# Decoder layer on one core: residual x1 kept in seven tiles of 128 tokens in place of eight of 112

## The chip, the cores and the metric

One NeuronCore of a Trainium2 chip runs the whole kernel. The metric is the device time of one execution in microseconds (us), the median of several.

## The reference

One pre-norm decoder layer on x of shape 8 x 112 x 512 (896 tokens) in float32, with a context of 8 x 375 x 512:

```python
x = x + attn(ln(x))                      # 16 heads of 32, rotary, causal, Wqkv with bias
x = x + xattn(ln(x), ctx)                # ln once more, with weights; then
    # q, k, v = fp8 linears of the tokens (16, 8, 8 heads of 128), LN per head, GQA within a sequence
    # qx = fp8 linear of the tokens; kx, vx = linear of ctx, LN on qx and kx, GQA over the 375
    # out = (fp8-rounded concat of both, 4096) @ wproj.T * scale
x = x + ffn(ln(x))                       # ternary weights, per group of 64
    # h = silu(gate) * up (2048); rms_norm(h) @ w_proj.T
```

The output is a float32 tensor of 8 x 112 x 512.

## The kernel before

The 896 tokens are worked on by batch: `NB` = 8 sequences of `T` = 112 tokens. The residual `x1` lies in SBUF as eight blocks of 112 partitions x 512. Where a matmul has the tokens as its weight columns, there are 112 of them, and the matmul streams 512 columns.

Phase A (up to about 225 us, `run_a`) normalises each batch, does its causal attention, adds it to x1 (`a_s4`, L640), normalises again (`l_0` to `l_2`) and quantises the tokens for the four linears (`l_q`, `quant`). Beside it the weights of S0 are prepared (`s0prep`): SP fetches blocks of 512 KB into four staging buffers, ACT casts them to bf16 (`b_0`, L326 and L328), and DVE or POOL forms the low part (`b_1`, L337 and L339).

The main loop goes by ticks. It runs four halves: S0 and S1 (self-attention by groups, heads 0 to 7 and 8 to 15) and X0 and X1 (the same over the context). A batch takes four ticks in S and eight in X. `p_mm` projects the tokens (L845, L855), `lnb_z` and `lnb_t` normalise and transpose (L785, L796), `t_s0` makes scores and exponentials (L935, L942, L947, L950), `t_s1` scales (L967), `t_s2` transposes and copies (L979, L996), `t_s3` multiplies by v (L1014), `t_s4` quantises four heads at a time into the buffer `cat` (`quant`: four DVE operations L655 to L658, then two on POOL, L659 and L660), and `t_s6` projects `cat` of a batch by 16 matmuls of 512 columns (L1052) and adds the result to x1 (L1058). Each stage runs a fixed number of ticks behind the first (`order`): `t_s4` five, `t_s6` eight. The weights of the next half are prepared in the same ticks, in X0 and X1 also the ternary weights of the FFN, half of which go out to DRAM through `spill_ring` and come back.

The FFN: `f_0` to `f_2` normalise and transpose x1 batch by batch (L1071, L1080, L1089, L1090) as soon as X1 has finished a batch; the first six come together after the last projection of queries. `g_0` and `g_1` do gate and up for 448 tokens at a time, 16 blocks of each (`j` = 0 among the last batches of X1, then `j` = 1): L1119, Silu on ACT L1128, product L1137, high and low part L1139 and L1140, squares summed on POOL L1145 and L1146. `d_0` and `d_1` do the down projection of a batch by 32 matmuls of 512 columns (L1168), its RMS factor (L1173, L1176, L1179) and the last sum (L1184), and SP stores it.

The order on each engine is the order in which the program emits: five queues, each strictly in order, with semaphores between them. SP has one queue, `sync_items`; an entry that waits holds up all behind it (`run_dma`).

Of the kernel before, what the change touches and what calls it, by code (L numbers as in the profile page):

```python
# [120 lines left out]
def decoder_layer(nc, x, ctx_t, w_a, w_s, w_x, w_p, w_g, w_d, vec, bias, cst, cst2, scr, out):  # L121
    ctx = ExitStack()
    with ctx:
# [59 lines left out]
        aFR = rings.take(1024)  # L183
        fr = Ring([f32(aFR + 512 * i, 512) for i in range(2)])
# [6 lines left out]
        catr = Ring([b16(rings.take(448), 896).rearrange("p (h t) -> p h t", h=8) for _ in range(2)])  # L191
# [263 lines left out]
        x1tok = [None] * NB  # L455
        A = [dict(b=b) for b in range(NB)]
# [167 lines left out]
        def a_s4(g):  # L624
# [17 lines left out]
            x1tok[b] = t3  # L642

# [5 lines left out]
        def quant(src, mul, dst, toks, free_dst):  # L649
# [10 lines left out]
            t5 = pool(lambda e: e.tensor_tensor(dst, t3, m3, ALU.subtract), t4, free_dst)  # L660
# [33 lines left out]
        def l_q(it, vs, last):  # L694
# [3 lines left out]
            for v in vs:  # L698
                dst = xqx[:, :, T * b:T * b + T] if v == 3 else xqv[:, v, :, T * b:T * b + T]
                mul = rsc[:, 4 * v:4 * v + 4].unsqueeze(2).broadcast_to([128, 4, T])  # L700
                t1, t5 = quant(f3, mul, dst, [tf, t_rsc], None)
# [104 lines left out]
        def proj_items():  # L806
            items = []
            for hf in halves:
                for b in range(NB):
                    bt = dict(hf=hf, b=b, ready=[], k=hf["kind"])  # L810
                    hf.setdefault("batches", []).append(bt)
                    bt["n"] = 4 if hf["kind"] == "S" else 8
# [210 lines left out]
        def t_s4(it):  # L1023
# [4 lines left out]
            if g == 1:  # L1028
                bt["cat"] = catr.take()
                bt["tcat"] = []  # L1030
            _, cat, cfree = bt["cat"]
# [5 lines left out]
            t1, t5 = quant(bk[:, 0:448].rearrange("p (h t) -> p h t", h=4), mul, cat[:, h0:h0 + 4, :],  # L1037
                           [it["tpv"], t_rsm], cfree)
            bank.release(bi, t1)
            bt["tcat"].append(t5)  # L1040

        def t_s6(it):
            if not it["last"]:
# [12 lines left out]
            catr.release(ci, t)  # L1056
# [4 lines left out]
            x1tok[b] = t2  # L1061
# [6 lines left out]
        def f_0(b):  # L1068
            si, rr, tr = ln_rstd(ln_stats(x1[:, b, :], T, 1, 512, x1tok[b]))
            zi, z, zf = zr.take()  # L1070
            th = act(lambda e: e.activation(z[0:T, :], x1[0:T, b, :], ACT.Identity, bias=rr[0:T, 1:2],  # L1071
                                            scale=rr[0:T, 0:1]), tr, zf, x1tok[b])
# [3 lines left out]
        def f_1(b):  # L1076
            zi, z, th = F[b]
            bi, (bk, _), free = bank.take()
            for k in range(4):
                t = pe(lambda e, k=k: e.transpose(bk[:, T * k:T * k + T], z[0:T, 128 * k:128 * k + 128],  # L1080
                                                  identf[0:T, 0:T]), th, free, signal=k == 3)
# [3 lines left out]
        def f_2(b):  # L1085
            bi, bk, t = F[b]
            b4 = bk[:, 0:448].rearrange("p (k t) -> p k t", k=4)
            sl = slice(T * b, T * b + T)
# [7 lines left out]
        ffn_h = [[], []]  # L1096
        spots = [
            [PW[0] + 3584 + 224 * m for m in range(16)],
            [PW[0] + 7168 + 224 * m for m in range(4)] + [X_CT + 224 * m for m in range(6)]
            + [X_K0 + 224 * m for m in range(6)],  # L1100
            [PW[0] + 8192 + 224 * m for m in range(16)],
            [aKV + 224 * m for m in range(13)] + [X_V0 + 224 * m for m in range(3)],
        ]
        for j in range(2):
            ffn_h[j] = [(b16(spots[2 * j][m], 448), b16(spots[2 * j + 1][m], 448)) for m in range(16)]
        acc = [f32(aXQX, 448), f32(a_att, 448)]
        sq = Ring([f32(aXQX + 448, 448)])
        hf_ring = Ring([f32(aXQX + 896 + 448 * i, 448) for i in range(2)] + [f32(X_V0 + 672, 448)])
        wg = b16(PW[1], 4 * 4096).rearrange("p (k n) -> p k n", k=4)
        wd = b16(PW[1] + 8192, 16 * 512).rearrange("p (m n) -> p m n", m=16)  # L1110
        def g_0(it):
            m, j = it["m"], it["j"]
            toks = [t for b in range(4 * j, 4 * j + 4) for t in xTtok[b]]
            for which in range(2):
                bi, (bk, _), free = bank.take()
                n = 0
                for k in range(4):
                    for s in range(2):
                        t = pe(lambda e, k=k, s=s, n=n, bk=bk, which=which: e.matmul(  # L1119
                            bk[:, 0:448], wg[:, k, 2048 * which + 128 * m:2048 * which + 128 * m + 128],  # L1120
                            xT[:, s, k, 448 * j:448 * j + 448], start=n == 0, stop=n == 7),
# [4 lines left out]
            i, h, hfree = hf_ring.take()  # L1126
            after = free_at[j]
            ts = act(lambda e: e.activation(h, bk[:, 0:448], ACT.Silu), t, hfree, after)  # L1128
# [3 lines left out]
        def g_1(it):  # L1132
# [4 lines left out]
            th = dve(lambda e: e.tensor_tensor(h, h, bk[:, 0:448], ALU.mult), t, it["ts"])  # L1137
# [5 lines left out]
            else:  # L1143
                qi, q, qf = sq.take()
                tq = pool(lambda e: e.tensor_tensor(q, h, h, ALU.mult), th, qf, after)  # L1145
# [12 lines left out]
        outs = []  # L1158

        def d_0(it):  # L1160
            b = it["b"]
            j = b // 4
            sl = slice(T * (b % 4), T * (b % 4) + T)
# [237 lines left out]
```

How the kernel before makes its waits and increments, by code:

```python
    def emit(self, eng):  # L63
        for need, make, inc in self.items:
            last = {}
            for t in need:
                last[id(t.sem)] = t
            for t in last.values():
                eng.wait_ge(t.sem, t.value)
            ins = make(eng)
            if inc:
                ins.then_inc(self.sem, 1)
# [1229 lines left out]
        def run_dma(eng, items):  # L1302
            for waits, dst, src, s in items:
                for t in waits:
                    eng.wait_ge(t.sem, t.value)
                eng.dma_start(dst, src).then_inc(s, 16)
# [1 line left out]
        @block.sync  # L1308
        def _(eng):
            run_dma(eng, sync_items)
            eng.wait_ge(s_out, 16 * NB)
```

## Time and profile before

| | |
|---|---|
| median of 3 runs | 1261.43 us (1261.06 to 1262.6) |
| profiled execution, its own time | 1259.75 us |
| its span | 1257.9 us |
| granted clock of TensorE, mean | 0.977 |
| PE, DVE, ACT, POOL busy | 95%, 75%, 64%, 48% of the span |
| HBM | 51 GB/s on average |

PE is TensorE's matmul stream and PEld its weight loads, DVE is VectorE, POOL is GpSimd, SP issues the DMAs. Records of matmuls overlap, as one starts before the one ahead of it has drained; their distance from start to start is what a stream costs. In a timeline the columns are start (us), length (us), engine, line, operation, output, input, count, and in brackets how long the engine had stood idle and what ended that. In the view by stretch they are the stretch, its length, then each engine's busy us with the number of instructions, the granted clock, the share of the DMA engines and GB/s. The view of a line gives count, ns at least, median and at most, first and last start. A DMA line ends with KB of one and median us from issue to landing.

### The profile page before, as it was taken

The page shows a single profiled execution, that of the slowest core. Times are in us where ns is not written, and L with a number is a line of the kernel's source. Part 1 is how long each engine was busy: PE and PEld are TensorE (multiplying, and loading weights), DVE is VectorE, ACT ScalarE, POOL GpSimd, SP SyncE. Part 2 cuts the span into 40 slices and gives each one's busy share as a digit, 9 for nine tenths or more (in the row PEclk, how much of TensorE's full clock was granted, in tenths as well). Part 3 has the DMA queues.
Part 4 walks back from the last instruction along what each step waited for, and adds up shares of the span by engine and source line. Part 5 has one row for each costly group of instructions (what it writes and reads, how often), then busy time and mean ns, then how long its engine had stood idle before and what let it go on. Part 6 is the DMA issues. An engine that isn't in the chain of part 4 may idle for free.

```text
span 1257.9 us, 19385 instructions
## 1 busy us (share of the span) xinstructions
PE 1195.8 (95%) x6408; PEld 819.4 (65%) x6432; DVE 938.0 (75%) x2794; ACT 805.3 (64%) x2301; POOL 607.8 (48%) x722
## 2 busy tenths in 40 slices
PE   4999989889999999999999999999999997999998
PEld 2677767566676666667666677766767765565545
DVE  4679987999888887899999866667777877463341
ACT  4676557777877776577666675667777767652230
POOL 2538875643544545465455632224544443363470
PEclk9999988899999999999999999999999999899999
DMA  8230000011211121212323211041101100000000
GB/s 264 86 99 18 2 1 1 1 51 51 67 35 34 59 80 47 92 44 91 104 88 109 82 47 38 17 142 59 50 27 59 59 18 1 1 1 16 15 1 30
DMA packets 25460, 65.60 MB, mean 52 GB/s; under 512 B 2720, under 2 KB 8992, under 8 KB 25360
## 3 DMA queue, kind: packets, MB, share of 16 engines
q1 hardware_dynamic: 25088, 64.00, 16.2%
q8 instruction: 51, 0.84, 0.3%
q14 instruction: 49, 0.40, 0.1%
q10 hardware_dynamic: 272, 0.36, 0.1%
HBM read 59.37 MB, written 4.98 MB: 51 GB/s over the span
## 4 chain that ended last, share of the span: by engine, by line
PE 47%; DVE 27%; ACT 19%; POOL 4%; issue 2%; DMA 1%; ACTq 0%; POOLq 0%; SPq 0%
PE ps L855 9%; PE ps L1052 8%; PE ps L1119 8%; ACT big L785 6%; PE ps L845 4%; PE ps L1168 4%; PE ps L1014 3%; PE ps L947 3%; DVE big L412 3%; DVE big L967 3%; ACT big L950 2%; PE ps L979 2%; DVE big L240 2%; DVE big L655 2%; DVE big L656 2%
## 5 line engine op out<-in xcount | busy, mean ns | idle before, releaser
L855 PE MATMUL ps<-big 128*125 128x512 bf16 x1152 | 264.5, 379 | 0.5 <-ACT big L942 0.5
L785 ACT ACTIVATE big<-ps,big 112x128 f32<-112x128 f32 (+1 forms) x512 | 192.4, 456 | 72.6 <-POOL big L430 70.1
L855 PEld LDWEIGHTS ps<-big 128*125 128x125 bf16 x1152 | 155.2, 136 | 80.3 <-ACT big L942 0.8
L429 POOL TENSOR_TENSOR big<-big 112x4 f32<-112x4 f32 (+1 forms) x128 | 38.6, 302 | 319.7 <-ACT big L424 319.7
L845 PE MATMUL ps<-big 128*112 128x512 bf16 x768 | 187.4, 387 | 1.9 <-ACT big L942 1.0
L659 POOL TENSOR_TENSOR big<-big 128x448 f32<-128x448 bf16 x96 | 102.8, 1071 | 111.1 <-DVE big L964 70.1
L845 PEld LDWEIGHTS ps<-big 128*112 128x112 bf16 x768 | 99.8, 132 | 65.8 <-issue 6.4
L967 DVE TENSOR_SCALAR big<-big 112x112 f32<-112x112 f32 (+1 forms) x256 | 131.5, 534 | 6.8
L412 DVE BATCH_NORM_STATS2 big<-ps 112x6 f32<-112x128 f32 (+1 forms) x512 | 113.3, 283 | 20.1 <-PE ps L855 18.8
L1014 PE MATMUL ps<-big 125*128 125x224 f32 (+1 forms) x512 | 122.1, 362 | 5.5 <-DVE big L996 4.8
L950 ACT ACTIVATE big<-ps,big 112x375 f32<-112x375 f32 x128 | 74.6, 583 | 82.3 <-DVE big L949 81.2
L1052 PE MATMUL ps<-big 128*112 128x512 bf16 x512 | 116.0, 379 | 3.2 <-ACT big L942 3.2
L660 POOL TENSOR_TENSOR big<-big 128x448 bf16<-128x448 f32 x96 | 111.6, 1163 | 7.5
L947 PE MATMUL ps<-big 128*112 128x375 f32 x256 | 103.5, 486 | 0.5 <-DVE big L657 0.5
L1014 PEld LDWEIGHTS ps<-big 125*128 125x128 f32 (+1 forms) x512 | 92.9, 194 | 16.7 <-DVE big L996 5.9
L979 PEld LDWEIGHTS ps<-big 112*125 112x125 f32 (+1 forms) x512 | 79.6, 177 | 29.0 <-DVE big L967 3.8
L1119 PE MATMUL ps<-big 128*128 128x448 bf16 x512 | 98.3, 352 | 0.0
L949 DVE TENSOR_REDUCE big<-ps 112x1 f32<-112x375 f32 x128 | 68.3, 534 | 39.1 <-PE ps L947 38.2
L1052 PEld LDWEIGHTS ps<-big 128*112 128x112 bf16 x512 | 65.3, 130 | 48.7 <-issue 7.8
L802 ACT ACTIVATE big<-ps,big 128x448 f32<-128x448 f32 (+1 forms) x128 | 94.3, 737 | 0.0
L979 PE MATMUL ps<-big 112*125 112x112 f32 (+1 forms) x512 | 85.7, 269 | 2.7 <-DVE big L967 1.5
L504 PE MATMUL ps<-big 128*112 128x512 bf16 x288 | 76.4, 415 | 5.1 <-DVE big L240 3.5
(115 smaller groups left out, 2312.4 us busy)
## 6 DMA issues: line engine op xcount, KB each, us to landing
big<-in_ctx_t SPq DMA_DIRECT2D x32, 375.0 KB, 3.7
big<-in_w_s SPq DMA_DIRECT2D x16, 512.0 KB, 3.6
big<-in_w_p SPq DMA_DIRECT2D x16, 512.0 KB, 3.7
big<-in_w_x SPq DMA_DIRECT2D x16, 512.0 KB, 3.8
big<-in_w_g SPq DMA_DIRECT2D x16, 512.0 KB, 3.7
big<-in_w_d SPq DMA_DIRECT2D x8, 512.0 KB, 4.6
big<-in_w_a SPq DMA_DIRECT2D x8, 384.0 KB, 4.6
scr<-big SPq DMA_DIRECT2D x24, 128.0 KB, 1.7
```

What stands on the lines that cost most here:

```text
L412: t = dve(lambda e, j=j: e.bn_stats(st[:, j, :], src[0:rows, width * j:width * j + width]), toks, free)
L659: t4 = pool(lambda e: e.tensor_tensor(t3, y3, m3, ALU.add), t2)
L660: t5 = pool(lambda e: e.tensor_tensor(dst, t3, m3, ALU.subtract), t4, free_dst)
L785: t = act(lambda e, j=j: e.activation(z[0:rows, 128 * j:128 * j + 128], bk[0:rows, 128 * j:128 * j + 128], ACT.Identity, bias=rr[0:rows, 4 ...
L845: t = pe(lambda e, k=k, s=s, n=n: e.matmul(bk[0:T, :], xq[:, k, :], w[:, s, k, col:col + 512], start=n == 0, stop=n == 7), xq_tok[(v, b)], ...
L855: t = pe(lambda e, k=k, s=s, u=u, n=n: e.matmul(bk[0:CK, :], cT[:, s, k, CK * c:CK * c + CK], w[:, u, k, col:col + 512], start=n == 0, sto ...
L947: t = pe(lambda e: e.matmul(bk[0:T, 0:SC], q[:, h, :], kk[:, g, :], start=True, stop=True), bt["ready"], free)
L967: tl = dve(lambda e, j=j: e.tensor_scalar(hl[0:T, w * j:w * j + w], p[0:T, w * j:w * j + w], ri[:, j:j + 1], None, ALU.mult), tr, hf)
L979: t = pe(lambda e, j=j: e.transpose(bb[0:rows, T * j:T * j + T], hl[0:T, rows * j:rows * j + rows], identf[0:T, 0:T]), it["tl"], free, sig ...
L1014: t = pe(lambda e, c=c: e.matmul(bk[:, o:o + 224], v[0:rows, c, 128 * g:128 * g + 128], pT[0:rows, 224 * c:224 * c + 224], start=c == 0, s ...
L1052: t = pe(lambda e, h=h, s=s, n=n: e.matmul(bk[0:T, :], cat[:, h, :], hf["wp"][:, s, h, :], start=n == 0, stop=n == 15), bt["tcat"], free, ...
L1119: t = pe(lambda e, k=k, s=s, n=n, bk=bk, which=which: e.matmul(bk[:, 0:448], wg[:, k, 2048 * which + 128 * m:2048 * which + 128 * m + 128] ...
```

## The change

After phase A has finished a batch of x1, SP stores it to a DRAM buffer `xs` of 896 x 512. Once the stores that cover 128 rows have landed and the old block has been read, it loads them into `x1t`, seven tiles of 128 tokens in the same SBUF. The attention stays by batches of 112; `quant` can write to several places, and `t_s4` writes the heads of a batch to one or two tiles of `cat` (two on POOL for batches 1 to 6). `t_s6` projects tile b-1 at the end of batch b, so nothing at the end of batch 0. There are three `cat` buffers in S and two in X. The FFN's norm, its down projection and the stores of the output go by these seven tiles; gate and up take 512 and 384 tokens in place of 448 and 448. The third `cat` buffer is the place of x1's eighth block, later used for the spill ring and for an FFN buffer.

```diff
-        aFR = rings.take(1024)
-        fr = Ring([f32(aFR + 512 * i, 512) for i in range(2)])
+        aFR = rings.take(896)
+        fr = Ring([f32(aFR + 448 * i, 448) for i in range(2)])
+        aCX = aX1 + 7 * D
+        x1t = f32(aX1, 7 * D).rearrange("p (i d) -> p i d", i=7)
...
+        aCat = [rings.take(512), rings.take(512), aCX]
+        cats = [b16(a, 1024).rearrange("p (h t) -> p h t", h=8) for a in aCat]
...
+            xs_tok[b] = load(sync_items, xs[T * b:T * b + T, :], x1[0:T, b, :], s_xs[b], 16, t3)
...
+            for dst, lo, hi, free_dst in dsts:
+                t5 = pool(lambda e, dst=dst, lo=lo, hi=hi: e.tensor_tensor(
+                    dst, t3[:, :, lo:hi], m3[:, :, lo:hi], ALU.subtract), t4, free_dst)
...
+            it["x1read"] = [it["st"]["t"], th]
+            if b:
+                i = b - 1
+                xttok[i] = load(sync_items, x1t[:, i, :], xs[128 * i:128 * i + 128, :], s_xl[i], 16,
+                                xs_tok[i], xs_tok[b], A[i]["x1read"])
...
+            for i, at, lo, hi in ((b - 1, 128 - 16 * b, 0, 16 * b), (b, 0, 16 * b, T)):
+                if not 0 <= i < NB - 1:
+                    continue
+                at = at if i < b else 0
+                if i not in hf["cat"]:
+                    slot = cat_n[0] % (3 if S else 2)
+                    cat_n[0] = 0 if hf["name"] == "S1" and i == NB - 2 else cat_n[0] + 1
+                    hf["cat"][i] = dict(slot=slot, free=cat_free[slot], toks=[])
+                pieces.append((hf["cat"][i], at, lo, hi))
+            if b == NB - 1:
+                pieces = [(hf["cat"][b - 1], 16, 0, T)]
+            t1, t5 = quant(bk[:, 0:448].rearrange("p (h t) -> p h t", h=4), mul,
+                           [(cats[p["slot"]][:, h0:h0 + 4, at:at + hi - lo], lo, hi, p["free"])
+                            for p, at, lo, hi in pieces], [it["tpv"], t_rsm])
...
+            if not it["last"] or not bt["b"]:
                 return
-            bt, hf = it["bt"], it["hf"]
-            b = bt["b"]
-            ci, cat, _ = bt["cat"]
+            i = bt["b"] - 1
+            tile = hf["cat"][i]
...
-                        bk[0:T, :], cat[:, h, :], hf["wp"][:, s, h, :], start=n == 0, stop=n == 15),
-                        bt["tcat"], free, ready[hf["name"] + "p"][h // 4], signal=n == 15)
+                        bk, cat[:, h, :], hf["wp"][:, s, h, :], start=n == 0, stop=n == 15),
+                        tile["toks"], free, ready[hf["name"] + "p"][h // 4], signal=n == 15)
...
-                x1[0:T, b, :], bk[0:T, :], pscale[0:T, :], x1[0:T, b, :], ALU.mult, ALU.add), t, t_ps, x1tok[b])
+                x1t[:, i, :], bk, pscale, x1t[:, i, :], ALU.mult, ALU.add), t, t_ps, xttok[i])
...
-            si, rr, tr = ln_rstd(ln_stats(x1[:, b, :], T, 1, 512, x1tok[b]))
+            si, rr, tr = ln_rstd(ln_stats(x1t[:, b, :], 128, 1, 512, xttok[b]))
...
+        W = (512, 384)
...
-            toks = [t for b in range(4 * j, 4 * j + 4) for t in xTtok[b]]
+            n0, w = 512 * j, W[j]
+            toks = [t for b in ((0, 1, 2, 3), (4, 5, 6))[j] for t in xTtok[b]]
...
-                            bk[:, 0:448], wg[:, k, 2048 * which + 128 * m:2048 * which + 128 * m + 128],
-                            xT[:, s, k, 448 * j:448 * j + 448], start=n == 0, stop=n == 7),
+                            bk[:, 0:w], wg[:, k, 2048 * which + 128 * m:2048 * which + 128 * m + 128],
+                            xT[:, s, k, n0:n0 + w], start=n == 0, stop=n == 7),
...
-            sl = slice(T * (b % 4), T * (b % 4) + T)
+            sl = slice(128 * (b % 4), 128 * (b % 4) + 128)
...
-                        bk[0:T, :], h[:, sl], wd[:, m, :], start=n == 0, stop=n == 31),
+                        bk, h[:, sl], wd[:, m, :], start=n == 0, stop=n == 31),
...
-            outs.append(load(sync_items, out[b], x1[0:T, b, :], s_out, 16 * (b + 1), t))
+            outs.append(load(sync_items, rows[128 * b:128 * b + 128, :], x1t[:, b, :], s_out, 16 * (b + 1), t))
...
-        spill_ring = Ring([f32(aFR + 256 * i, 256) for i in range(4)])
+        spill_ring = Ring([f32(a, 256) for a in (aFR, aFR + 256, aCX, aCX + 256)])
...
-                free_rings((catr, pr, hlr, ptr), all_now())
+                free_rings((pr, hlr, ptr), all_now())
+                cat_free[:] = [all_now()] * 3
...
-                spill_ring.free = [[t for f in fr.free for t in f]] * 4
+                spill_ring.free = [all_now()] * 4
...
-                for b in range(NB):
-                    if tick == lag + max(n_items + b // 2, n_items - 64 + 8 * b + LEAD + 16):
+                for b in range(NB - 1):
+                    if tick == lag + max(n_items + b // 2, n_items - 64 + 8 * (b + 1) + LEAD + 16):
...
-        drain(pipeline([dict(b=b) for b in range(4, NB)], [(1, d_1), (0, d_0)]))
+        drain(pipeline([dict(b=b) for b in range(4, NB - 1)], [(1, d_1), (0, d_0)]))
```

## Rows read from the trace of the kernel before

**Rows 1.** The page, part 1: busy us (share of the span) and instructions.
```profile
PE 1195.8 (95%) x6408; PEld 819.4 (65%) x6432; DVE 938.0 (75%) x2794; ACT 805.3 (64%) x2301; POOL 607.8 (48%) x722
```

**Rows 2.** Busy time by stretch: S0, X0, X1 and the turn to the FFN.
```profile
278.80:295.70 16.90, 16.08 (x92) 11.02 (x93) 15.51 (x59) 13.24 (x43) 6.76 (x10) 1.00 0.20 64
567.00:601.00 34.00, 33.63 (x173) 23.58 (x174) 31.21 (x96) 24.43 (x64) 19.12 (x23) 1.00 0.23 77
866.00:899.80 33.80, 33.69 (x174) 23.91 (x175) 25.76 (x89) 24.11 (x66) 15.72 (x21) 1.00 0.18 55
1053.40:1077.30 23.90, 16.11 (x69) 12.16 (x68) 14.91 (x35) 17.32 (x49) 2.06 (x2) 0.79 0.00 0
```

**Rows 3.** Timeline of PE: a projection group in S0 and what follows.
```profile
278.81 3.63 PE L1052 MATMUL ps<-big 128*112 128x512 bf16 x16 [0.34 <-ACT big L942]
282.28 0.54 PE L1014 MATMUL ps<-big 112*128 112x224 f32 x2
```

**Rows 4.** Timeline of DVE behind batch 0's group in S0, S1, X0.
```profile
265.58 0.75 DVE L1058 SCALAR_TENSOR_TENSOR big<-ps,big 112x512 f32<-112x512 f32 x1
267.89 0.39 DVE L996 COPY big<-ps 112x224 f32<-112x224 f32 x1 [0.89 <-PE ps L979]
...
399.16 0.39 DVE L996 COPY big<-ps 112x224 f32<-112x224 f32 x1 [1.55 <-PE ps L979]
...
568.34 1.79 DVE L240 TENSOR_TENSOR big<-big 128x750 bf16<-128x750 f32 x2 [0.76 <-ACT big L239]
580.26 0.29 DVE L366 TENSOR_SCALAR big<-big 128x512 bf16<-128x512 bf16 x1 [1.04 <-ACT big L356]
```

**Rows 5.** Timeline of ACT and PE: the sixth norm tile.
```profile
1069.00 0.28 ACT L423 ACTIVATE big<-big 112x1 f32<-112x1 f32 x1
1070.10 0.81 ACT L1071 ACTIVATE big<-big 112x512 f32<-112x512 f32 x1
1070.97 1.01 PE L1080 MATMUL ps<-big 112*128 112x112 f32 x4 [1.23 <-ACT big L1071]
```

**Rows 6.** Timeline of PE: tiles of the down projection.
```profile
1140.60 8.80 PE L1168 MATMUL ps<-big 128*112 128x512 bf16 x32 [2.51 <-DVE big L1140]
...
1232.32 7.09 PE L1168 MATMUL ps<-big 128*112 128x512 bf16 x32
1239.37 7.09 PE L1168 MATMUL ps<-big 128*112 128x512 bf16 x32
```

**Rows 7.** Timeline of PE: a stretch of gate and up matmuls.
```profile
1179.68 4.51 PE L1119 MATMUL ps<-big 128*128 128x448 bf16 x23
```

**Rows 8.** Line L1119: xcount, ns min/median/max, first and last start.
```profile
L1119 PEld LDWEIGHTS ps<-big x512: 95/98/168, 1077.0 to 1222.4; 128*128 128x128 bf16 x171
L1119 PE MATMUL ps<-big x512: 349/352/355, 1077.3 to 1222.6; 128*128 128x448 bf16 x171
```

**Rows 9.** Timeline of DVE and ACT around L640; DMA issues of in_w_p.
```profile
75.21 1.13 DVE L640 TENSOR_TENSOR big<-big 112x512 f32<-112x512 f32 x1
80.10 0.69 DVE L337 TENSOR_TENSOR big<-big 128x512 bf16<-128x512 f32 x1 [1.27 <-ACT big L326]
79.45 1.14 ACT L326 ACTIVATE big<-big 128x512 bf16<-128x512 f32 x2
big<-in_w_p SPq DMA_DIRECT2D x16, 512.0 KB, 3.7
```

**Rows 10.** POOL: line L660, DVE: line L967, POOL's timeline of L429.
```profile
L660 POOL TENSOR_TENSOR big<-big x96: 1030/1036/2777, 95.7 to 1137.7; 128x448 bf16<-128x448 f32 x96
L967 DVE TENSOR_SCALAR big<-big x256: 264/415/1367, 217.3 to 1113.0; 112x112 f32<-112x112 f32 x64, 112x375 f32<-112x375 f32 x64
262.28 0.70 POOL L429 TENSOR_TENSOR big<-big 112x4 f32<-112x4 f32 x1 [3.38 <-ACT big L424]
275.28 0.20 POOL L429 TENSOR_TENSOR big<-big 112x4 f32<-112x4 f32 x1 [2.21 <-ACT big L424]
```

**Rows 11.** Line L1052: its weight loads.
```profile
L1052 PEld LDWEIGHTS ps<-big x512: 126/130/132, 261.9 to 1152.4; 128*112 128x112 bf16 x171
```

More of the change, by code:

```diff
@@ L455, in decoder_layer @@
         x1tok = [None] * NB
+        s_xs = [sem(f"s_xs{b}") for b in range(NB)]
+        s_xl = [sem(f"s_xl{i}") for i in range(NB - 1)]
+        xs_tok, xttok = [None] * NB, [None] * (NB - 1)
         A = [dict(b=b) for b in range(NB)]
@@ L811, in proj_items @@
                     hf.setdefault("batches", []).append(bt)
+                    hf.setdefault("cat", {})
                     bt["n"] = 4 if hf["kind"] == "S" else 8
@@ L1027, in t_s4 @@
                 return
[L1028 to L1031, printed above, removed]
+            b = bt["b"]
             bi, (bk, _), _ = it["ob"]
@@ L1036, in t_s4 @@
             mul = rsm[:, col:col + 4].unsqueeze(2).broadcast_to([128, 4, T])
-            t1, t5 = quant(bk[:, 0:448].rearrange("p (h t) -> p h t", h=4), mul, cat[:, h0:h0 + 4, :],
-                           [it["tpv"], t_rsm], cfree)
+            pieces = []
+            for i, at, lo, hi in ((b - 1, 128 - 16 * b, 0, 16 * b), (b, 0, 16 * b, T)):
[12 more added lines that the diff above has]
+                            for p, at, lo, hi in pieces], [it["tpv"], t_rsm])
             bank.release(bi, t1)
-            bt["tcat"].append(t5)
+            for p, at, lo, hi in pieces:
+                p["toks"].append(t5)
+        cat_free, cat_n = [[], [], []], [0]
         def t_s6(it):
-            if not it["last"]:
+            bt, hf = it["bt"], it["hf"]
+            if not it["last"] or not bt["b"]:
                 return
-            bt, hf = it["bt"], it["hf"]
-            b = bt["b"]
-            ci, cat, _ = bt["cat"]
+            i = bt["b"] - 1
+            tile = hf["cat"][i]
+            cat = cats[tile["slot"]]
             bi, (bk, _), free = bank.take()
@@ L1068, in f_0 @@
         def f_0(b):
-            si, rr, tr = ln_rstd(ln_stats(x1[:, b, :], T, 1, 512, x1tok[b]))
+            si, rr, tr = ln_rstd(ln_stats(x1t[:, b, :], 128, 1, 512, xttok[b]))
             zi, z, zf = zr.take()
-            th = act(lambda e: e.activation(z[0:T, :], x1[0:T, b, :], ACT.Identity, bias=rr[0:T, 1:2],
-                                            scale=rr[0:T, 0:1]), tr, zf, x1tok[b])
+            th = act(lambda e: e.activation(z, x1t[:, b, :], ACT.Identity, bias=rr[:, 1:2], scale=rr[:, 0:1]),
+                     tr, zf, xttok[b])
             small.release(si, th)
@@ L1096, in decoder_layer @@
         ffn_h = [[], []]
+        W = (512, 384)
         spots = [
[L1098 to L1102, printed above, removed]
+            [PW[0] + 3584 + 256 * m for m in range(16)],
+            [PW[0] + 7680 + 256 * m for m in range(2)] + [X_CT + 256 * m for m in range(5)]
+            + [X_K0 + 256 * m for m in range(5)] + [X_V0 + 256 * m for m in range(4)],
+            [PW[0] + 8192 + 192 * m for m in range(16)],
+            [aKV + 192 * m for m in range(15)] + [PW[0] + 11264],
         ]
         for j in range(2):
[L1105 to L1108, printed above, removed]
+            ffn_h[j] = [(b16(spots[2 * j][m], W[j]), b16(spots[2 * j + 1][m], W[j])) for m in range(16)]
+        acc = [f32(aXQX, 512), f32(a_att, 384)]
+        sq = Ring([f32(aXQX + 512, 512)])
+        hf_ring = Ring([f32(a, 512) for a in (aXQX + 1024, aCX, X_V0 + 1024)])
         wg = b16(PW[1], 4 * 4096).rearrange("p (k n) -> p k n", k=4)
@@ L1126, in g_0 @@
             i, h, hfree = hf_ring.take()
+            h = h[:, 0:w]
             after = free_at[j]
-            ts = act(lambda e: e.activation(h, bk[:, 0:448], ACT.Silu), t, hfree, after)
+            ts = act(lambda e: e.activation(h, bk[:, 0:w], ACT.Silu), t, hfree, after)
             bank.release(bi, ts)
@@ L1158, in decoder_layer @@
         outs = []
+        rows = out.rearrange("b t d -> (b t) d")
         def d_0(it):
```

38 lines of the change are left out of this document (19 added, 19 removed).

## The prediction

> **What bounds the kernel now.** I read the page's first part first. The profiled execution spans 1257.9 us (1259.75 as timed), and PE is busy for 95% of it [rows 1]. That share belongs to several stages, so I cut the span into stretches, and the reader should compare PE, DVE and ACT in each [rows 2]. A batch of the self-attention half S0 has PE at 16.08 of 16.9 us, with DVE at 15.51 right behind. A batch of X0 has PE at 33.63 of 34.0 and DVE at 31.21. A batch of X1 has PE at 33.69 of 33.80 with DVE and ACT about a quarter idle. Then come 24 us in which PE works for only 16 at a granted clock of 0.79, between the last projection of queries and the first gate matmul. So PE is the limit from X1 on, except in those 24 us; in S0, S1 and X0 it is PE with DVE close behind. What a saved matmul is worth depends on which of these stretches it comes from.
>
> Then I looked for the price of a matmul with 512 columns in a full stream. In PE's order of time, 16 of L1052 start at 278.81 and what follows starts at 282.28: 3.47 us, 0.217 each [rows 3]. The 0.379 us of one record in the grouped view is latency, most of it under the next matmul. The third look was at what DVE waits for just after a removed matmul group, since that is all the time DVE can give back. The last were the queues that the edit touches: SP's early on, POOL's throughout.
>
> **The change part by part.**
>
> *Output projections.* Eight groups of 16 matmuls in each of four halves become seven; each stays at 512 columns. The group of batch 0 goes. On PE that is 4 x 3.47 = 13.9 us. What comes late in its place is DVE's work of the same tick, so each half is taken by itself; DVE also loses one eviction at L1058, 0.75 us. [rows 4] has DVE's waits in those batches.
> - S0: DVE stands still for 0.89 us behind the group (until L979 delivers). 0.89 + 0.75 = 1.64. Ends: 0.75 and 3.47.
> - S1: 1.55 + 0.75 = 2.30, same ends.
> - X0: two waits of 0.76 and 1.04 in the batch, with 0.75 that is 2.55, same ends.
> - X1: DVE has 25.76 and ACT 24.11 of 33.80 us [rows 2]: the whole 3.47. Low end 2.5.
>
> Sum 9.96; between 4.8 and 13.9.
>
> *Norm ahead of the FFN.* Eight tiles become seven. Two still come late, among the gate matmuls; six become five in the stretch at clock 0.79. The one that leaves is the second of a pair: ACT's chain for it runs from 1069.00 to 1070.91, and PE waits 1.23 us for its end [rows 5]. I take 1.8, near ACT's 1.91, because PE next waits for that same queue. Ends: 0.5 (PE would wait for something else) and 1.9.
>
> *Down projection.* Tiles 4 to 7 become 4 to 6. In the last stretch one tile follows another after 7.05 us (1232.32 to 1239.37) with no wait [rows 6]. One fewer is 7.05; low end 6.5, since the last store carries 256 KB for 224.
>
> *Gate and up.* 448 + 448 columns become 512 + 384, 256 matmuls each. At 448 the pitch is (4.51 - 0.352) / 22 = 0.189 us, 0.422 ns per column [rows 7, 8]; at 512 0.217, 0.424 ns. A constant price per column gives 0.162 at 384: +7.1 us in the first part, -6.9 in the second, so 0. Ends: -0.4 and, if 384 columns cost what 448 do, +6.9. DVE, ACT and POOL have the same elements in total.
>
> *Stores to xs and loads back.* Fifteen DMAs join SP's queue in order. Most stand where SP has nothing urgent: S1's first weights queue behind them, but are first used four ticks after the last of these, about a batch of S0, 16.9 us. One place is tight. The store of batch 0 waits for L640 (75.21 + 1.13 = 76.34), and the last three of S0's projection weights are behind it; ACT took the first of them at 79.45, without a wait for a DMA. New: issue near 77, 3.7 us to landing as for in_w_p, so about 80.7, and up to 82 with the store's 224 KB ahead. ACT comes 1.2 to 2.5 late; behind it DVE's L337 already waits 1.27 us at 80.10 for ACT, and ACT's next work waits for DVE, so nothing absorbs it [rows 9]. I take 1.6, ends 0 and 3.7 (a whole landing).
>
> *Quantised heads cut in two.* In six of eight batches both subtractions L660 of a batch become two operations: 48 more on POOL. The elements stay the same, so each costs the fixed part. The smallest POOL operations give the price: 112x4 took 0.20 us at one place and 0.70 at another [rows 10]. PE needs the result three ticks later, some 12 us (a tick of S0 is a quarter of 16.9), which hides 0.2 to 0.7. But the same rows have L967 on DVE between 0.264 and 1.367 us and L660 between 1.030 and 2.777: the two hold each other up. In S0, S1 and X0 (36 of the 48, 7.2 us of POOL) DVE has little room. I take 1.0, nearer to 0 than to 7.2, because most L660 run at their shortest (median 1.036). In X1 DVE's idle quarter hides it.
> Of the Trainium skill, "SBUF — State Buffer", section "Who interferes with whom", speaks against this edit: GpSimd and VectorE share one pair of ports, and whoever has it holds it for a whole instruction while the other fully blocks. The spread of both lines agrees. By that rule taken at its worst the whole 7.2 us would fall on DVE and the sum would be 10.0 in place of 16.2.
>
> *Costed at nothing.* The three (then two) buffers for cat: a slot is freed by matmuls that PE has queued ahead of those the quantisation waits for anyway. The reload of x1t is needed at the first projection of S0, at 278.81, while tile 0's store can go at 76.34. The spill ring's wait on all engines comes once, at the end of a tick, on ACT, which idles a quarter of that time; without that cover an estimate is a quarter of a tick, 1 us. Evictions and norms of 128 rows cost what those of 112 do, as the length per row is the same. PE's clock: the wait of 2.51 us at 1140.60 goes ahead of a tile that takes 8.80 us in place of 7.09 [rows 6]; that wait grows by some 0.3 and may cost the same again or not, 1.7 us either way, counted 0.
>
> **Sum:** 9.96 + 1.8 + 7.05 - 1.6 - 1.0 = 16.2 us. 1259.75 - 16.2 = 1243.5. The median of the three runs is 1.68 us above the profiled execution, so 1245.
>
> **Rivals.**
> - *DVE gives nothing back in S0, S1 and X0.* For: DVE at 92% of a batch in S0 and X0. Against: the waits in rows 4. Without 6.5 us of the sum: 1252.
> - *384 columns cost what 448 do.* Against: the price per column is the same at 448 and 512. 6.9 us worse: 1252. Both of these together: 1258.6, about no change.
> - *PE's whole saving comes through.* For: PE has the highest share everywhere. 13.9 for 9.96, without the two costs: 1238.7.
> - *Weight loads count.* Every projection and down matmul now loads 128 columns. A load of 128 took 0.098 us where one of 112 took 0.130 [rows 8, 11]. If that lay on the path, 672 x 0.032 = 21.5 us more would go: 1224. Against: 0.217 for 512 and 0.189 for 448 are the same per column, though the loads differ.
> The Trainium skill, "TensorE: Matmul & The Clock Gate", section "Weight-path perf modes", says that the fast load is on where there are 128 weight columns and the type isn't fp32. The two durations agree with it; that it would shorten a stream of 512 columns, no row shows.
> - *Slower: POOL's pieces block DVE.* Place: L660 in all halves. Price: 0.70 us each on the path, 48 x 0.70 = 33.6. For: that 0.70 and the longest L967. Against: POOL idles half of the span. It outweighs the gain of 17.2 from 0.36 us per piece on; at 0.70 the time is 1278.
>
> **How the numbers follow.** The forecast has 0.61, with its own range 1241 to 1249 (DVE's share, clock and SP wait at either end). DVE gives nothing back 0.13; 384 as dear as 448 0.05; both 0.03; the whole saving 0.10; weight loads 0.03; slower 0.05. From 1238 to 1254 the first, second, third and fifth of these fit, 0.89 less their tails. A difference below 0.2%, 2.5 us, can't be told from none: faster 0.92, same 0.03 (both costs together), slower 0.05.
>
> **What would show it.** L1052 448 times, L1168 224 times, still 0.217 apart. The last tiles 7.05 us apart, three in number. L1119 at about 0.162 in its second half. In S0's first batch no group at L1052, and PE waiting for DVE in its place; in X1 no such wait. In phase A ACT idle at L326 for a DMA of in_w_p. L660 with pieces of 64 to 384 elements, their sum per pair about 0.2 us above 1.036, and L967 little longer than before. The prediction falls if the time from S0's first projection to the last eviction of X1 shrinks by less than 5 us, if a POOL piece costs 0.36 us on the path, or if the last stretch keeps its length.

## The result

The changed kernel takes 1249.01 us (median of 4, 1248.66 to 1249.16) against 1261.24 before: 12.2 us less, ratio 0.990 with a 95% interval of 0.9883 to 0.9918. In the rounds of a later comparison it was 1248.72 against 1260.57, 11.9 less, ratio 0.9905 (0.9892 to 0.9919). Forecast were 1245, with a range of 1238 to 1254. The profiled executions differ by 10.6 us of span (1257.94 and 1247.37), and the marks below are theirs: the one of the kernel before was 1.5 us faster than its median, the other at its median, so the marks explain 10.6 of the 12.2 us.

The page of the changed kernel answers to [rows 1]:

```profile
PE 1177.8 (94%) x6330; PEld 782.0 (63%) x6330; DVE 934.7 (75%) x2785; ACT 804.9 (65%) x2295; POOL 619.6 (50%) x769
```

PE has lost 18 us of its records and POOL gained 12, DVE has 3 less. Where the time went is read from marks on PE that both kernels have; the table holds the length of each piece (us), all from starts in PE's timeline (the last mark is the span's end).

| piece | before | after | difference | forecast |
|---|---|---|---|---|
| start to the projection at the end of S0's batch 1 | 278.81 | 279.69 | +0.88 | -0.04 (+1.6 phase A, -1.64) |
| S0 batch 7 to S1 batch 1 | 32.45 | 31.15 | -1.30 | -2.30 |
| S1 batch 3 to 4 | 19.56 | 18.57 | -0.99 | 0 |
| S1 batch 7 to X0 batch 1 | 79.97 | 79.95 | -0.02 | -2.55 |
| X0 batch 1 to batch 7 | 223.67 | 223.96 | +0.29 | +1.0 in all halves, for POOL's pieces |
| X0 batch 7 to X1 batch 1 | 75.06 | 73.18 | -1.88 | -3.47 |
| X1 batch 5 to the first gate matmul | 27.36 | 24.61 | -2.75 | -1.8 |
| from there to the first down tile | 63.30 | 71.60 | +8.30 | +7.1 |
| from there to the second part of gate and up | 33.78 | 33.52 | -0.26 | 0 |
| the second part, to down tile 4 | 50.89 | 43.82 | -7.07 | -6.9 |
| from there to the end | 32.67 | 27.00 | -5.67 | -7.05 |

The other pieces differ by 0.1 us in sum. Much came as forecast. The groups kept their price, and the gate matmuls of 384 columns cost what a constant price per column gives: 113 of them in 18.53 us, 0.163 each. The view by line and form shows the counts:

```profile
L1081 PE MATMUL ps<-big 128*128 128x512 bf16 x448 | 101.2, 379 | 2.6 <-ACT big L957 2.6
L1150 PE MATMUL ps<-big 128*128 128x384 bf16 x256 | 41.8, 326 | 0.0
L1202 PE MATMUL ps<-big 128*128 128x512 bf16 x224 | 52.5, 395 | 6.0 <-DVE big L1172 6.0
```

```profile
1199.78 18.53 PE L1150 MATMUL ps<-big 128*128 128x384 bf16 x113
```

POOL's pieces cost their fixed part and no more: L668 (L660 before) took 121.2 us in 144 operations against 111.6 in 96, so 0.20 us for each of the 48 additional ones. By form, a piece of 64 elements and a whole block:

```profile
L668 POOL TENSOR_TENSOR big<-big 128x64 bf16<-128x64 f32 x16 | 6.1, 379 | 0.6
L668 POOL TENSOR_TENSOR big<-big 128x448 bf16<-128x448 f32 x48 | 55.1, 1147 | 3.8
```

In phase A, ACT waits for the fetch behind the store, and DVE's L340 for ACT; these two answer to [rows 9]:

```profile
82.25 1.15 ACT L329 ACTIVATE big<-big 128x512 bf16<-128x512 f32 x2 [2.37 <-DMA big<-in_w_p]
82.91 0.69 DVE L340 TENSOR_TENSOR big<-big 128x512 bf16<-128x512 f32 x1 [3.75 <-ACT big L329]
```

ACT takes the block 2.8 us later than before, and the last step of batch 1's attention (L646, L640 before) starts 24.10 us after batch 0's in place of 21.62. In other executions of kernels with this order it started 23.3 to 23.9 after, so the wait costs 1.7 to 2.5 at its place. Phase A as a whole is longer by as much: from the end of batch 0's L646 to the end of the last one, eight executions with this order took 148.5 to 150.0 us (mean 149.2), and three of kernels without the stores 146.8 to 147.9 (mean 147.2).

In X0 the group of batch 0 is gone, and PE waits for DVE in its place, at 560.48, 562.79, 570.31 and 598.50. These waits eat the gain step by step: counted from S1's last projection, the first multiplication by v behind the group's place (L1029, L1014 before) starts 2.2 us earlier than before the change, the next one 1.1, the two after that 0.55 each, and the one behind batch 1's projection at the same time. In X1 PE waits once for ACT, and ACT ahead of that for POOL. The two DVE rows answer to the last two of [rows 4]:

```profile
560.48 0.58 PE L994 MATMUL ps<-big 112*125 112x112 f32 x3 [0.59 <-DVE big L982]
562.79 1.40 PE L1029 MATMUL ps<-big 125*128 125x224 f32 x6 [1.10 <-DVE big L1011]
570.31 1.40 PE L1029 MATMUL ps<-big 125*128 125x224 f32 x6 [0.77 <-DVE big L1011]
598.50 0.58 PE L994 MATMUL ps<-big 112*125 112x112 f32 x3 [0.79 <-DVE big L982]
872.56 0.89 PE L962 MATMUL ps<-big 128*112 128x375 f32 x2 [0.60 <-ACT big L799]
...
566.86 1.79 DVE L243 TENSOR_TENSOR big<-big 128x750 bf16<-128x750 f32 x2 [1.42 <-ACT big L242]
578.79 0.29 DVE L369 TENSOR_SCALAR big<-big 128x512 bf16<-128x512 bf16 x1 [1.05 <-ACT big L359]
...
871.00 1.51 ACT L799 ACTIVATE big<-ps,big 112x128 f32<-112x128 f32 x4 [1.57 <-POOL big L433]
```

At the end, PE's waits ahead of the first and the fifth down tile, and the tiles behind them, answer to [rows 6]; the stretch below is from the view by stretch:

```profile
1143.03 8.49 PE L1202 MATMUL ps<-big 128*128 128x512 bf16 x32 [3.92 <-DVE big L1172]
...
1220.37 8.75 PE L1202 MATMUL ps<-big 128*128 128x512 bf16 x32 [2.06 <-DVE big L1172]
...
1222.00:1224.00 2.00, 2.00 (x7) 0.63 (x6) 0.00 (x0) 0.00 (x0) 0.00 (x0) 0.50 0.00 0
```

Tile 4 took 8.75 us where one without a wait takes 7.07: in the middle of it the granted clock is 0.50, the lower of the two levels, 1.2 GHz, after PE had stood for 2.06 us. Before the change the same place, with 2.30 us of waiting, kept the full clock.

### The profile page after: what moved, and what is told of

The parts are those of the page before. It is cut to its first block, busy times and chain, and to the rows that moved or that the text cites. A ratio compares the mean times of both kernels' runs of the same rounds, so it can differ in the third digit from the quotient of the medians.

```text
span 1247.4 us, 19243 instructions
## 1 busy us (share of the span) xinstructions
PE 1177.8 (94%) x6330; PEld 782.0 (63%) x6330; DVE 934.7 (75%) x2785; ACT 804.9 (65%) x2295; POOL 619.6 (50%) x769
## 4 chain that ended last, share of the span: by engine, by line
PE 57%; DVE 26%; ACT 11%; POOL 3%; issue 2%; DMA 1%; ACTq 0%; POOLq 0%; SPq 0%
PE ps L870 14%; PE ps L1150 8%; PE ps L1081 7%; PE ps L860 6%; PE ps L1029 5%; PE ps L962 4%; PE ps L1202 4%; DVE big L982 3%; DVE big L415 3%; ACT big L799 3%; PE ps L994 3%; PE ps L810 2%; DVE big L662 2%; DVE big L663 2%; DVE big L342 2%
## 5 line engine op out<-in xcount | busy, mean ns | idle before, releaser
L432 POOL TENSOR_TENSOR big<-big 112x4 f32<-112x4 f32 (+1 forms) x128 | 38.5, 301 | 311.2 <-ACT big L427 311.2
L860 PE MATMUL ps<-big 128*112 128x512 bf16 x768 | 188.9, 390 | 4.3 <-ACT big L957 1.7
L860 PEld LDWEIGHTS ps<-big 128*112 128x112 bf16 x768 | 100.3, 133 | 69.8 <-issue 7.9
L982 DVE TENSOR_SCALAR big<-big 112x112 f32<-112x112 f32 (+1 forms) x256 | 133.5, 542 | 6.8
L1029 PE MATMUL ps<-big 125*128 125x224 f32 (+1 forms) x512 | 121.3, 359 | 3.9 <-DVE big L1011 3.1
L668 POOL TENSOR_TENSOR big<-big 128x448 bf16<-128x448 f32 (+6 forms) x144 | 121.2, 855 | 7.5
L1081 PE MATMUL ps<-big 128*128 128x512 bf16 x448 | 101.2, 379 | 2.6 <-ACT big L957 2.6
L1029 PEld LDWEIGHTS ps<-big 125*128 125x128 f32 (+1 forms) x512 | 91.6, 192 | 16.2 <-DVE big L1011 5.1
L1150 PE MATMUL ps<-big 128*128 128x512 bf16 (+1 forms) x512 | 98.3, 352 | 0.0
L510 PE MATMUL ps<-big 128*112 128x512 bf16 x288 | 75.7, 412 | 4.9 <-DVE big L243 4.1
L1150 PEld LDWEIGHTS ps<-big 128*128 128x128 bf16 x512 | 50.1, 98 | 45.9 <-issue 0.4
```

What stands on the lines that cost most here:

```text
L668: t5 = pool(lambda e, dst=dst, lo=lo, hi=hi: e.tensor_tensor(dst, t3[:, :, lo:hi], m3[:, :, lo:hi], ALU.subtract), t4, free_dst)
L860: t = pe(lambda e, k=k, s=s, n=n: e.matmul(bk[0:T, :], xq[:, k, :], w[:, s, k, col:col + 512], start=n == 0, stop=n == 7), xq_tok[(v, b)], ...
L982: tl = dve(lambda e, j=j: e.tensor_scalar(hl[0:T, w * j:w * j + w], p[0:T, w * j:w * j + w], ri[:, j:j + 1], None, ALU.mult), tr, hf)
L1029: t = pe(lambda e, c=c: e.matmul(bk[:, o:o + 224], v[0:rows, c, 128 * g:128 * g + 128], pT[0:rows, 224 * c:224 * c + 224], start=c == 0, s ...
L1081: t = pe(lambda e, h=h, s=s, n=n: e.matmul(bk, cat[:, h, :], hf["wp"][:, s, h, :], start=n == 0, stop=n == 15), tile["toks"], free, ready[ ...
```

## The experiments

The theory after this look: what the removed groups give back is set by DVE, ACT and POOL's older operations beside DVE's, not by the new pieces on POOL; the phase A loss is SP's queue order; and the end loses to the wait and the clock. The rival for X0 and X1: the pieces took it.

The kernel before took 1261.24 us beside the changed kernel, but 1260.01 in the rounds of e1 to e4, 1260.04 in those of e5 to e8, and 1260.57 in those of e9 to e11. So a time is also compared with before in its own rounds, where the changed kernel is 11.9 to 12.2 us faster. The intervals of e1, e3, e4, e5 and e8 overlap that of the changed kernel: what these five show is read from marks and rows, not from the whole time. In the traces of e1, e3, e4 and e9 to e11 some matmul records are missing, often the first of a group, which shifts a mark by 0.2 us; a mark of theirs is best compared with another of theirs.

**e1_late_store.** The store of batch 0 is entered behind S0's last fetches: stores and reloads go to a list of their own, which joins the queue at `n` = 20.

```diff
-            xs_tok[b] = load(sync_items, xs[...
+            xs_tok[b] = load(xq[0], xs[...           # xq[0]: a list of its own up to tick 20
...
+            if n == 20:
+                sync_items.extend(xq[0])
+                xq[0] = sync_items
```

> The changed kernel, with the store of batch 0's x1 entered in SP's queue behind the last three fetches of S0's projection weights instead of ahead of them; nothing else moves. Theory (the queue order alone costs the 2.5 us by which S0 now starts late): ACT no longer waits for in_w_p in phase A, S0's first projection group starts near 277.2 us instead of 279.7, and the time falls by 2.5 us to about 1246.5. Rival (it is the traffic of the stores and reloads, or slower work of other engines): no change, 1249.

Measured: 1247.69 us (1246.12 to 1249.25). ACT takes the block at 79.88 and names no wait:

```profile
79.88 1.14 ACT L329 ACTIVATE big<-big 128x512 bf16<-128x512 f32 x2
```

The last step of batch 1's attention starts 21.62 us after batch 0's again, so the order in the queue is the cause of the wait. But S0's batch 1 is projected at 278.63, only 1.1 us earlier, and the time is 1.0 to 1.3 lower, or 0.1 to 0.5 against before in its own rounds. The 2.5 us of the theory did not come. Phase A ran at another granted clock (0.87 from 120 to 160 us, 1.00 in the changed kernel's profile) and lost 1.1 us between batches 3 and 4; the kernel before had 0.91 there without that loss, so the clock isn't shown to be its reason. From batch 0's L646 to the last one e1 and e9, which has the same order, took 148.2 and 148.0 us, against 149.2 in the mean with the early store. The cause of the wait is shown; of the 2.0 us by which phase A is longer, the late store gave back about 1.1, and the other 0.9 is not explained.

**e2_before_less.** The kernel before, without the projection of batch 0.

```diff
+            if b == 0:
+                catr.release(ci, *bt["tcat"])
+                return
```

> The kernel before, with the projection of batch 0 and its addition to x1 left out in all four halves (this part of the computation is missing); tiles of 112 everywhere else. Theory (what a group of 3.47 us on PE gives back is set by DVE and ACT in that batch, and in X0 nothing comes back): S0 1.6, S1 1.3 to 2.3, X0 0 to 0.5, X1 1.9 us, together 5 to 6, so about 1255.5. Rival 1 (the two-piece subtractions on POOL took the gain from X0 and X1 in the changed kernel): without them X0 gives 2.55 and X1 3.47, together 10, so 1251. Rival 2 (PE's whole time comes back): 13.9, so 1247.5.

Measured: 1255.23 us against 1260.01 before, ratio 0.996 (0.9945 to 0.9975): 4.8 us. By the marks S1 gives 1.5 us, X0 none (79.98 for 79.97), X1 1.87 (73.19). S0 gives 1.7, counted from the last L640 to the projection of batch 1 (53.49 for 55.23). PE's waits in X0 are those of the changed kernel to 0.1 us:

```profile
559.16 0.58 PE L979 MATMUL ps<-big 112*125 112x112 f32 x3 [0.59 <-DVE big L967]
561.47 1.40 PE L1014 MATMUL ps<-big 125*128 125x224 f32 x6 [1.10 <-DVE big L996]
568.99 1.40 PE L1014 MATMUL ps<-big 125*128 125x224 f32 x6 [0.76 <-DVE big L996]
597.22 0.58 PE L979 MATMUL ps<-big 112*125 112x112 f32 x3 [0.84 <-DVE big L967]
```

There are no pieces in this kernel, so rival 1 falls: what a group gives back is the same without them. PE's whole time (rival 2) falls too.

**e3_one_piece.** One piece per block in place of two; three fills of cat are added.

```diff
+            if len(pieces) == 2:
+                pieces = [(pieces[1][0], 0, 0, T)]
```

> The changed kernel, with each quantised block written in one piece to the tile of its own batch, so that the last 16 to 112 tokens of a tile hold what lay there (this part of the computation is wrong); three fills of the cat buffers are added on POOL once. 48 pieces fewer on POOL. Theory (the pieces cost next to nothing): within 1 us of the changed kernel, 1248 to 1249.5. Rival (the pieces block DVE and took the gain in X0 and X1): 4 to 7 us faster, 1242 to 1245.

Measured: 1250.76 us (1248.78 to 1251.85), S1 to X0 79.97. Not faster, so the rival falls, and the 1.0 us of the forecast finds no support. But the time is 1.3 us above the theory's range, and 2.6 to 3.0 slower than the changed kernel when each is set against before in its own rounds. The three fills can have a part in that; the trace, of its fastest execution, doesn't show where it was lost.

**e4_more_pieces.** Every piece cut again.

```diff
-                t5 = pool(... dst, t3[:, :, lo:hi], m3[:, :, lo:hi], ALU.subtract ...
+                for k in ((0, 2), (2, 4)):
+                    t5 = pool(... dst[:, k[0]:k[1]], t3[:, k[0]:k[1], lo:hi], m3[:, k[0]:k[1], lo:hi] ...
```

> The changed kernel, with every piece of the last subtraction in the attention's quantisation cut again in two (two heads each): 112 operations more on POOL, the same elements. Theory (a piece costs its fixed part on POOL, which is hidden): less than 2.5 us slower, at most 1251.5. Rival (each piece is on the path with its 0.20 us): 22 us slower, 1271; at a third of that 1256.

Measured: 1246.79 us (1245.25 to 1247.30), about 2 us less than the changed kernel, or 1.0 to 1.4 against before in its own rounds. The theory's bound holds and the rival falls; that 112 more operations would make it faster, neither foresaw. In X0 projections 1, 2 and 3 follow each other after 37.6 us in place of 38.2 (the later ones are as far apart as before, or 0.5 us further), and in this profile the wait ahead of the first down tile is 3.01 us in place of 3.92. The timelines of DVE and POOL just ahead of X0's projection 1 show how. In the changed kernel:

```profile
591.90 1.95 POOL L668 TENSOR_TENSOR big<-big 128x64 bf16<-128x64 f32 x2
593.81 1.35 POOL L372 TENSOR_TENSOR big<-big 128x512 bf16<-128x512 bf16 x1
...
594.18 1.53 DVE L370 SCALAR_TENSOR_TENSOR big<-big 128x512 bf16<-128x512 bf16 x1
597.12 1.33 DVE L982 TENSOR_SCALAR big<-big 112x375 f32<-112x375 f32 x1
```

and with more pieces:

```profile
592.17 2.61 POOL L669 TENSOR_TENSOR big<-big 128x32 bf16<-128x32 f32 x4
594.74 1.60 POOL L372 TENSOR_TENSOR big<-big 128x512 bf16<-128x512 bf16 x1
...
594.40 0.92 DVE L370 SCALAR_TENSOR_TENSOR big<-big 128x512 bf16<-128x512 bf16 x1
596.73 1.12 DVE L983 TENSOR_SCALAR big<-big 112x375 f32<-112x375 f32 x1
```

POOL's pieces end 0.9 us later (0.7 against what goes ahead of them), so L372 on POOL starts behind DVE's L370 and not ahead of it. L370 then takes 0.92 us for 1.53, and the scaling that PE waits for (L982, here L983) ends at 597.85 in place of 598.45. This is a matter of who meets whom: over 600 to 750 us the mean of that scaling is not shorter (0.692 us for 0.620), and yet PE's wait at the end of each of these batches is gone.

**e5_fill.** Matmuls that nobody reads in the two waits.

```diff
+            if b in (0, 4):
+                ui, (uk, _), ufree = bank.take()
+                for q in range(14 if b == 0 else 8):
+                    tu = pe(... e.matmul(uk, wd[:, 0, 0:128], wd[:, 1, :], start=True, stop=True), ufree, ready["d"])
+                bank.release(ui, tu)
```

> The changed kernel, with matmuls of 512 columns whose result nobody reads put ahead of the first down tile of each half (14 before tile 0, 8 before tile 4), where PE waits 3.92 and 2.06 us for the last block of the FFN's hidden layer; both fit into the waits (3.0 and 1.7 us). Theory (those two tiles take 8.3 and 8.6 us instead of 6.95 because PE's clock falls in the wait): both take 6.95 again, 3 us faster, about 1246. Rival (the tiles are long for another reason, such as late data): they stay long, 1249 or a little slower.

Measured: 1246.38 us (1245.46 to 1247.76), 2.3 to 2.6 less, or 1.4 to 1.8 against before in its own rounds; 3 were expected. Both tiles take 7.08 us with the fill in front of them:

```profile
1142.45 7.08 PE L1208 MATMUL ps<-big 128*128 128x512 bf16 x32 [0.36 <-DVE big L1172]
...
1218.30 7.08 PE L1208 MATMUL ps<-big 128*128 128x512 bf16 x32 [0.24 <-DVE big L1172]
```

The data they read come no earlier in this kernel, so it was the clock that made them long.

**e6_wait_by_block and e7_before_by_block.** The same edit on the changed kernel and on the one before.

```diff
-                        hd[j], free, ready["d"], signal=n == 31)
+                        hd[j][2 * m:2 * m + 2], free, ready["d"], signal=n == 31)
```

> The changed kernel, with each matmul of the down projection waiting for its own block of the hidden layer (16 blocks) instead of all sixteen ahead of the first. Theory (the two waits of 3.92 and 2.06 us and the falls of the clock that follow them, 1.4 and 1.6, are wholly on the path): 9 us faster, 1240. Rival (the last block is late whatever is ahead of it, so the wait only moves to the 31st matmul): 0 to 3 us faster, 1246 to 1249.

> The kernel before, with the same wait by block. Its waits are 2.51 and 2.30 us, with one fall of the clock, 1.7. Theory: 6.5 us faster than before, about 1254, so that the change in this form is worth 14 us, 2 more than as it stands, since the clock's fall at tile 4 came with the change. Rival (the clock's fall has nothing to do with what the change is worth): the change is worth the same 12 us in both forms.

Measured: 1239.71 us (ratio to before 0.9836, 0.9821 to 0.9850) and 1251.50 (0.9931, 0.9915 to 0.9948). Both waits are gone, and so are the long tiles; in the first:

```profile
1137.77 7.07 PE L1202 MATMUL ps<-big 128*128 128x512 bf16 x32
...
1211.47 7.07 PE L1202 MATMUL ps<-big 128*128 128x512 bf16 x32
```

The first gained 9.0 to 9.3 us, or 8.1 to 8.5 against before in the same rounds; 9 were expected. The second gained 8.5 where 6.5 were expected, and the change is worth 11.8 us in this form, as much as in the other: the theory of the second text falls and its rival stands. The waits and the clock cost both kernels alike, within what one execution differs from the next; they don't explain the shortfall.

**e8_x0_act.** X0's copies of the transposed probabilities on ACT.

```diff
-            if it["hf"]["name"] == "X1":
+            if it["hf"]["name"] in ("X0", "X1"):
```

> The changed kernel, with the copies of the transposed probabilities in X0 on ACT instead of DVE (as X1 has them). Theory (DVE paces X0, which is why nothing of batch 0's group came back there): a batch of X0 falls from 38.2 to 37.6 us and batch 0 gives back 1.5 to 3 us, together 2 to 5 us faster, 1244 to 1247. Rival (ACT, 24.4 of 34 us busy and 3.7 more then, comes late in its place; or PE's own work sets the pace): no change or up to 2 us slower.

Measured: 1250.12 us, 1.9 to 2.3 slower against before in its own rounds, X0's projections 1 to 3 38.5 us apart in place of 38.2. The theory as put there falls and the rival stands: less work for DVE doesn't help, since PE then waits for ACT too (0.7 and 0.4 us for the copies at L1009, between 560 and 600 us).

**e10_no_pool_add.** The weights' rounding without its two POOL operations.

```diff
-            t4 = pool(lambda e: e.tensor_tensor(m, m, a, ALU.subtract), t3)
-            t5 = pool(lambda e: e.tensor_tensor(m, m, a, ALU.add), t4)
-            u.update(t5=t5, m=m32, ti=ti)
+            u.update(t5=t3, m=m32, ti=ti)
```

> The changed kernel, with the two POOL operations of the FFN weights' rounding (a subtraction and an addition in X0 and X1) left out; the weights come out unrounded in part (this part of the computation is wrong). DVE, ACT and PE keep all their work. Theory (DVE is held by POOL's operations on the port they share, and that sets X0's pace): a batch of X0 falls from 38.2 to 37.6 us, batch 0 of X0 gives back 2 to 3.5 us in place of 0, and the time falls by 3 to 7 us, 1242 to 1246. Rival (DVE's own 31 of 34 us, or ACT, set the pace): X0 stays at 38.1 and batch 0 at 0; no change, 1249.

Measured: 1243.09 us against 1248.72 for the changed kernel in the same rounds. X0's projections 1 to 3 are 37.5 us apart, S1 to X0 takes 76.86 in place of 79.90, and X0 to X1 72.03 for 72.96 (both against the changed kernel in e11). One of the four waits in X0 is left:

```profile
567.65 1.40 PE L1027 MATMUL ps<-big 125*128 125x224 f32 x6 [0.76 <-DVE big L1009]
```

DVE has all its work in this kernel. What is gone is seen in the stretch from 600 to 636 us, here and then in the changed kernel: POOL is busy for 11.85 us in place of 20.25, and DVE for 32.22 in place of 33.11 with one instruction more.

```profile
600.00:636.00 36.00, 35.84 (x184) 24.66 (x186) 32.22 (x105) 26.17 (x69) 11.85 (x18) 1.00 0.29 89
```

```profile
600.00:636.00 36.00, 36.00 (x186) 24.82 (x184) 33.11 (x104) 26.77 (x68) 20.25 (x25) 1.00 0.30 92
```

So POOL's operations, those that were there before, set X0's pace. That they do it by holding DVE up, and not by a late result, is read from the lengths. At the place of batch 0's group DVE does the same work in the same order, first in the changed kernel, with L373 and L372 on POOL beside it, then here without them:

```profile
556.93 1.60 DVE L370 SCALAR_TENSOR_TENSOR big<-big 128x512 bf16<-128x512 bf16 x1
559.10 1.33 DVE L982 TENSOR_SCALAR big<-big 112x375 f32<-112x375 f32 x1
...
556.82 1.16 POOL L373 TENSOR_TENSOR big<-big 128x512 bf16<-128x512 bf16 x1
559.07 1.15 POOL L372 TENSOR_TENSOR big<-big 128x512 bf16<-128x512 bf16 x1 [1.09 <-DVE big L979]
```

```profile
556.10 0.69 DVE L370 SCALAR_TENSOR_TENSOR big<-big 128x512 bf16<-128x512 bf16 x1
557.35 0.41 DVE L980 TENSOR_SCALAR big<-big 112x375 f32<-112x375 f32 x1
```

The two take 2.93 us there and 1.10 here (L371 between them 0.42 in both), which is 1.8 of the 2.0 us that PE gains at this place. DVE shows no wait for POOL in that batch in either kernel, and its two waits for ACT are the same in both (1.4 and 1.0 us), as are ACT's for POOL's results (1.24, 0.68 and 0.30). Of the 3.0 us between S1 and X0, 2.0 are there behind the place of batch 0's group, and the last 1.0 comes ahead of projection 1, whose group is still in place: so at most 2.0 of the 3.47 us of batch 0's group came back, and the rest is X0's faster pace.

**e9_three and e11_after_again.** Late store, wait by block and finer pieces together, and the changed kernel beside it.

> The changed kernel with three edits together: the down projection waits by block, the store of batch 0's x1 comes behind S0's fetches in SP's queue, and the last subtraction of the attention's quantisation goes in pieces of two heads. Theory (the three are independent: 9.3, 2.4 and 2.5 us by the traces): 14 us faster than the changed kernel, about 1235. Rival (S0's later or earlier start shifts how DVE and POOL meet in X0, so that the pieces' gain goes): 1237 to 1238.

> The changed kernel as it is, on the chip and in the rounds of the two others, so that they can be compared with it directly. Theory: 1249 with before at 1261, or both about 1 us lower as in the other runs. The fall of PE's clock at the last down tiles may come or not from one execution to the next, 1.6 us.

Measured: 1235.99 us (1234.80 to 1236.64), ratio to before 0.9801 (0.9787 to 0.9814), and 1248.72 for the changed kernel. 12.7 us of the 14.0 came; X0's projections 1 to 3 are again 37.6 us apart, S0's start gained 0.4 us against the changed kernel in these rounds. This is the fastest version found, faster than both kernels.

## Why the prediction was right, and what was off

The direction and the range held, and so did the main idea: the 64 output and 32 down matmuls fewer are worth what the stage around each gives back. How X0 and X1 give back was read wrongly. The sum of 16.2 us was too large by 4, and the total flatters it: the output projections were 5 us short, the down projection and gate and up 1.2 to 1.4 each, while 1 us from the norm, 1 from POOL's pieces, and an unforeseen 1 us in S1 that stays unexplained came on top, which is luck. By its steps:

- *Output projections*, 9.96 forecast, 4.8 measured, which is the low end of the bounds. S0 was right (1.64; 1.4 to 1.7 from the last L640 on). S1 was 1.30 for 2.30. X0, 2.55, is the mis-sized term: it gave 0.0 (-0.02 and, in e2, 0.01). The step took DVE's waits of 0.76 and 1.04 in [rows 4] as time to be had. They are ended by ACT, where those of S0 and S1 are ended by PE, which comes earlier without the group. They stayed, at 1.42 and 1.05 us, and they are still there in e10, where time does come back: what can be had in X0 is not DVE's idle time but the length of its operations. e10 shows that POOL's two operations beside them are the cause, by giving back up to 2.0 us of 3.47 once they are gone. (The 34 us that the prediction calls a batch of X0 are a part of it; one takes 38.1.) X1, 3.47, gave 1.87: DVE and ACT have a quarter of their time free in the mean, but in that tick ACT waits 1.57 us for POOL's L433 and PE 0.60 for ACT; the matmuls around that wait start further apart, which takes the other 1.0. e10 has no such wait there. The mean share of a stretch was read as room in one tick of it.
- *Norm*, 1.8 forecast, 2.75 measured. In e2, without any change there, the same piece was 0.7 shorter, so about 2.1 belong to the tile and the rest to how the clock falls there.
- *Down projection*, 7.05 forecast. The tiles are 7.05 apart as before; tile 4 lost 1.7 of it to the clock in the profiled execution. That is chance as much as change: in e11 the same kernel has tile 4 at full clock and tile 0 longer.
- *Gate and up*, 0 forecast: +8.30 and -7.07. The wait ahead of tile 0 grew by 1.4 where 0.3 was allowed; the last L1172 on DVE took 1.56 us for 1.08 before; POOL's square L1178 starts 0.03 us ahead of it, so it looks held by POOL, which no run tested.
- *SP's queue*, 1.6 forecast, 1.7 to 2.5 measured at its place. Phase A is 2.0 longer in the mean, of which the late store gave back 1.1.
- *POOL's pieces*, 1.0 forecast, nothing measured; a piece is 0.20 us on POOL, as worked out. The rule of the Trainium skill that was weighed against the change ("SBUF — State Buffer", "Who interferes with whom") fits e10, in which L370 and L982 (L980 there) fall from 2.93 to 1.10 us without POOL's operations beside them; that it is the ports through which POOL holds DVE is the page's account, and no run separates it from another hold. The page limits it to DVE instructions that use the shared pair, which the prediction left out. But that hold was there before the change, and the pieces add nothing to it that e2 or e3 shows; cut finer, they even help.

Of the rivals, the nearest was the one in which DVE gives nothing back in S0, S1 and X0 (1252): it is 3 us from the measured time, the forecast 4, but it is true of X0 alone. A constant cost at 384 columns and weight loads are ruled out by the pitches, 0.217 at 512 and 0.163 at 384, PE's whole saving by e2, and the slower one by e3 and e4. One sign of failure can't be read as it was put: the time from S0's first projection to X1's last eviction also holds the first part of gate and up, which grew by 8.3 us.

What stays open: why S1's batch 3 to 4 was 1.0 us shorter after the change and 1.0 longer in e2, what slowed e3, and how much of phase A's wait reaches the end of the whole kernel.

## What to carry to other kernels

Price a removed instruction by the tick it leaves, with the chain that runs through it, and not by an engine's mean idle share over the stage: a wait in which the neighbour stands still is only to be had if what ends it moves as well. Look at what ends each wait (here PE, which moves with the removed group, or ACT, which does not) and at which of the neighbour's operations run long beside another engine. A consumer that reads sixteen blocks should wait block by block: one line there gave 8.5 us in the kernel before, about seven tenths of what the whole retiling gave.

## What the runs showed of the hardware that was not expected

- Waits of 2.06 to 3.92 us on PE are followed in some executions by a tile at the lower clock and in others not, at the same place in the same kernel: tile 4 took 8.75 us in one profile of the changed kernel, after 2.06 us, and about 7.1 in another (6.85 without its first record, which is missing), which had the longer tile at tile 0 (9.99 us there, 8.49 in the first).
- More and shorter operations on POOL brought X0's projections 1 to 3 0.6 us closer to each other, though POOL's busy time grew (21.41 us for 20.25 from 600 to 636): by the rows under e4, when POOL takes its next operation decides how long DVE's is held up.
- Two DVE operations took two to three times as long beside POOL's as without: L370 1.60 us for 0.69, L982 1.33 for 0.41 (changed kernel and e10).
